# Main loop with eight batches to a body instead of two, and the end of the angle features at later steps

## The reference

```
def _chunk_attn(...):                       # layers L0, L1, L3; L0 and L1 are followed by add and norm
    scores = einsum('bnqhd,bnkhd->bnhqk', qh, kh) * scale + mask   # chunks of 64, 8 heads
    out = einsum('bnhqk,bnkhd->bnqhd', softmax(scores), vh)
    return (out @ W_out.T + b_out) * masks

idx = top_k(2 p.p - xx - xx^T, 30)          # p: the context's positions; 30 nearest of 1024
rel = pts[idx] - pts                        # three coordinates of each neighbour
r2, sxy2 = ...; rho = sqrt(r2); sxy = sqrt(sxy2)
theta = arctan2(zr, sxy); phi = arctan2(yr, xr)
feat = concat(sph, sph - mean(sph))         # sph = (rho, theta, phi)
h = lrelu(bn(lrelu(bn(lrelu(bn(feat @ W1.T)) @ W2.T)) @ W3.T))   # batch norms over all 32 batches
att = softmax(h over the 30 neighbours)
out = norm(x + layers + sum(att * xk))
```

## Time and profile before

| | us |
|---|---|
| median of 3 runs (lowest to highest) | 6258.06 (6256.48 to 6260.03) |
| the profiled execution | 6258.18 |
| its span in the trace | 6256.4 |
| DVE busy | 5585.7 (89%) |
| PE busy | 5448.7 (87%) |
| ACT busy | 4490.2 (72%) |
| POOL busy | 3506.1 (56%) |

### The profile page before, as it was taken

One profiled execution on the slowest core, in us unless ns is written; L12 is line 12 of the kernel. 1 busy time (PEld: TensorE's weight loads), 2 busy tenths in 40 slices (PEclk: granted clock), 3 DMA queues, 4 the chain that ended last, 5 costly groups with the idle time before them and its releaser, 6 DMA issues. The chain is left out here.

```text
span 6256.4 us, 228198 instructions
## 1 busy us (share of the span) xinstructions
PE 5448.7 (87%) x82804; PEld 3392.0 (54%) x82804; DVE 5585.7 (89%) x7936; ACT 4490.2 (72%) x17146; POOL 3506.1 (56%) x3600
## 2 busy tenths in 40 slices
PE   7888888888888888888888888888859769999999
PEld 3455555555555555555555555555533357777776
DVE  7999999999999999999999999999945787777776
ACT  7888888888888888888888888888845623333333
POOL 4466666666666666666666666666670033333332
PEclk9999999999999999999999999999969889999999
DMA  2333333333333333333333333333323023333332
GB/s 46 95 94 110 90 99 98 94 97 95 95 107 98 96 108 91 100 98 93 97 92 99 107 98 94 110 90 100 88 101 75 0 72 96 85 88 85 89 93 72
DMA packets 656108, 568.86 MB, mean 91 GB/s; under 512 B 557824, under 2 KB 579584, under 8 KB 620960
## 3 DMA queue, kind: packets, MB, share of 16 engines
q1 hardware_dynamic: 618016, 284.53, 19.4%
q10 hardware_dynamic: 36864, 268.45, 12.1%
HBM read 384.78 MB, written 67.24 MB: 72 GB/s over the span
## 5 line engine op out<-in xcount | busy, mean ns | idle before, releaser
L769 ACT ACTIVATE prob<-SC,row_max 128x64 f32<-128x64 f32 x6144 | 1836.1, 335 | 376.6 <-DVE row_max L1123 368.0
L886 POOL TENSOR_TENSOR prob<-prob,row_rec 128x512 f32<-128x512 f32 x768 | 800.6, 1042 | 1379.4 <-DVE row_rec L1131 1369.3
L769 ACT ACTIVATION_READ_ACCUMULATOR prob<-SC,row_max 128x1 f32 x6144 | 1387.0, 228 | 0.0
L1115 DVE FIND_INDEX8 nbr<-top,dist 128x8 uint16<-128x1024 f32 x1024 | 1234.5, 1217 | 0.0
L1108 DVE MAX8 top<-dist 128x8 f32<-128x1024 f32 x1024 | 1190.4, 1203 | 1.5
L1110 DVE MATCH_REPLACE8 dist<-top,dist 128x1024 f32<-128x1024 f32 x768 | 923.6, 1207 | 0.0
L627 PE MATMUL SC<-k_bd,q_t 128*64 128x256 f32 x6144 | 877.4, 409 | 0.0
L1801 ACT ACTIVATE dense<-DM 128x512 f32<-128x512 f32 x512 | 305.4, 596 | 750.1 <-PE DM L1760 750.0
L1909 DVE TENSOR_TENSOR d_oh_a<-lo,iota_a 128x4096 bf16<-128x4096 bf16 x256 | 583.8, 2290 | 241.2 <-PE DM L1760 240.3
L648 PEld LDWEIGHTS PT<-ident,prob 128*128 128x128 f32 x3072 | 358.0, 144 | 791.9 <-issue 770.4
L589 PEld LDWEIGHTS G<-table,low_all 128*128 128x128 bf16 x24576 | 664.8, 96 | 169.1 <-issue 92.5
(11 more groups left out here) (216 smaller groups left out, 9463.1 us busy)
## 6 DMA issues: line engine op xcount, KB each, us to landing
low_all<-low_scratch ACTq DMA_DIRECT2D x256, 1024.0 KB, 4.8
k_bd<-k_t SPq DMA_DIRECT2D x3072, 16.0 KB, 1.9
placed<-compact SPq DMA_DIRECT2D x256, 192.0 KB, 3.9
ctx<-in_ctx SPq DMA_DIRECT2D x32, 512.0 KB, 3.3
mask<-in_mask SPq DMA_DIRECT2D x32, 512.0 KB, 8.8
xb<-in_x SPq DMA_DIRECT2D x32, 512.0 KB, 3.4
x_scratch<-xb SPq DMA_DIRECT2D x32, 512.0 KB, 4.0
y_scratch<-y_b SPq DMA_DIRECT2D x32, 512.0 KB, 6.7
```

Of the source, the lines that this page charges most:

```text
L769: last = act.activation(prob[:, s % 4, g * CHUNK:(g + 1) * CHUNK], SC[:, s % 2, g * CHUNK:(g + 1) * CHUNK], ACT.Exp, bias=row_max[:, s % 2 ...
L886: pool.tensor_tensor(pr, pr, row_rec[:, r % 2, :].unsqueeze(2).to_broadcast([128, 8, CHUNK]), ALU.mult).then_inc(normed, 1)
L1115: last = dve.max_index(nbr[:, uu % BPB, t, k * 8:(k + 1) * 8], best, row)
```

## The change

`BPB` becomes 8, and `BUFS` = 2 takes its place wherever it meant the number of buffers; `TURNS` = 4 is how often a body goes round them. The written-out first and last bodies now have 8 batches each, and the loop has 2 bodies of 8: it jumps back once. No spurious batch -1 arises, so the waits on `gram_ready` lose their 1. The turn moves from step 44 to 45, the signed angle from 45 to 46 and its DMA from 46 to 47, the centring from 46 to 50.

```diff
 KEY_BUFS = 3
-BPB = 2
+BPB = 8
+BUFS = 2
+TURNS = BPB // BUFS
 BODY = N // BPB
...
-RATIO_AT, ANGLE_AT, TURN_AT, SPH_AT, SPH_OUT_AT = 44, 44, 44, 45, 46
-RHO_OUT_AT, TYPICAL_AT, CENTRE_AT, GRAM_AT = 39, 42, 46, 54
+RATIO_AT, ANGLE_AT, TURN_AT, SPH_AT, SPH_OUT_AT = 44, 44, 45, 46, 47
+RHO_OUT_AT, TYPICAL_AT, CENTRE_AT, GRAM_AT = 39, 42, 50, 54
...
-        ctx = sb("ctx", [128, BPB, T])
+        ctx = sb("ctx", [128, BUFS, T])
...
-            eng.wait_ge(arrivals[u % BPB], START + (i + u // BPB + 1) * 16)
+            eng.wait_ge(arrivals[u % BUFS], START + (i * TURNS + u // BUFS + 1) * 16)
...
-            act.wait_ge(gram_ready, START + N + 1)
+            act.wait_ge(gram_ready, START + N)
...
-                    pool.wait_ge(gram_ready, START + b + 1)
+                    pool.wait_ge(gram_ready, START + b)
```

More of the change, by code:

```diff
@@ L220, in attention_and_neighbours @@
         oh_b = sb("oh_b", [128, NF, 8], BF16)
-        pts = sb("pts", [128, BPB, 3 * NT])
-        table = sb("table", [128, BPB, 3, 24], BF16)
+        pts = sb("pts", [128, BUFS, 3 * NT])
+        table = sb("table", [128, BUFS, 3, 24], BF16)
         left = sb("left", [128, 2, 24])
@@ L252, in attention_and_neighbours @@
         zeroed = sem("zeroed")
[L253 to L256, removed]
+        ctx_in = [sem(f"ctx_in{u}") for u in range(BUFS)]
+        x_in = [sem(f"x_in{u}") for u in range(BUFS)]
+        mask_in = [sem(f"mask_in{u}") for u in range(BUFS)]
+        by_chunk_in = [sem(f"by_chunk_in{u}") for u in range(BUFS)]
         pj_ready = sem("pj_ready")
@@ L260, in attention_and_neighbours @@
         cols_out = sem("cols_out")
-        cols_in = [sem(f"cols_in{u}") for u in range(BPB)]
-        pts_in = [sem(f"pts_in{u}") for u in range(BPB)]
+        cols_in = [sem(f"cols_in{u}") for u in range(BUFS)]
+        pts_in = [sem(f"pts_in{u}") for u in range(BUFS)]
         pool_split = sem("pool_split")
@@ L283, in attention_and_neighbours @@
         applied = [sem(f"applied{j}") for j in range(2)]
-        x2_out = [sem(f"x2_out{u}") for u in range(BPB)]
+        x2_out = [sem(f"x2_out{u}") for u in range(BUFS)]
         y3_out = sem("y3_out")
@@ L396, in mask_by_chunk @@
                                  chunks[h].broadcast_to([32, PAIRS, CHUNK])).then_inc(by_chunk_in[u], 16)
-            for u in range(BPB):
+            for u in range(BUFS):
                 sp.wait_ge(zeroed, START)
@@ L540, in _ @@
             alone(sp)
-            for u in range(BPB):
-                sp.wait_ge(x2_out[u], START + BODY * 16)
+            for u in range(BUFS):
+                sp.wait_ge(x2_out[u], START + N // BUFS * 16)
             sp.wait_ge(y3_out, START + N * 16)
@@ L573, in projection @@
                     for e in range(2):
-                        last = pe.matmul(bank[64 * e:64 * e + 64, m * 64:(m + 1) * 64], ctx[:, pu % BPB, t0:t0 + CHUNK],
+                        last = pe.matmul(bank[64 * e:64 * e + 64, m * 64:(m + 1) * 64], ctx[:, pu % BUFS, t0:t0 + CHUNK],
                                          w_v[:, e, :, :], start=True, stop=True)
@@ L588, in fetch @@
                     for part in range(3):
-                        last = pe.matmul(G[:, g * 24:(g + 1) * 24], hot[:, t % 2, col:col + 128], table[:, v % BPB, part, :],
+                        last = pe.matmul(G[:, g * 24:(g + 1) * 24], hot[:, t % 2, col:col + 128], table[:, v % BUFS, part, :],
                                          start=(part == 0), stop=(part == 2))
@@ L697, in square @@
                     act.wait_ge(dist_row_ready, START + i * BPB + ub)
-                act.activation(sq[:, :], ctx[:, ub % BPB, :], ACT.Square).then_inc(squared, 1)
+                act.activation(sq[:, :], ctx[:, ub % BUFS, :], ACT.Square).then_inc(squared, 1)
             def squares(i, ub, h):
@@ L849, in split_row @@
             def split_row(i, ub, part, prior):
-                row = dist_row[:, ub % BPB, :]
+                row = dist_row[:, ub % BUFS, :]
                 if prior is None:
@@ L912, in step @@
                     landed(pool, mask_in, i, uu)
-                    pool.tensor_tensor(mine, mine, mask[:, uu % BPB, half], ALU.mult).then_inc(y_masked, 1)
+                    pool.tensor_tensor(mine, mine, mask[:, uu % BUFS, half], ALU.mult).then_inc(y_masked, 1)
                 if real(i, r, STEPS) and r % 4 == 3 and place(r)[0] < 2:
@@ L1114, in neighbours @@
                             alone(dve)
-                        last = dve.max_index(nbr[:, uu % BPB, t, k * 8:(k + 1) * 8], best, row)
+                        last = dve.max_index(nbr[:, uu % BUFS, t, k * 8:(k + 1) * 8], best, row)
                         if op == "i3":
@@ L1184, in indices @@
                 alone(dve)
-                here = nbr[:, v % BPB, :, :].rearrange("p t k -> p (t k)")
+                here = nbr[:, v % BUFS, :, :].rearrange("p t k -> p (t k)")
                 dve.tensor_scalar(low_u[:, :], here, 127, None, ALU.bitwise_and)
```

58 lines of the change are left out of this document (29 added, 29 removed).

## The result

| | median, us (lowest to highest) | profiled execution | its span |
|---|---|---|---|
| before | 6259.05 (6256.48 to 6262.41), 4 runs | 6258.18 | 6256.4 |
| after | 6201.8 (6193.92 to 6206.81), 4 runs | 6204.94 | 6203.1 |

The ratio is 0.9907, with a 95% interval of 0.989 to 0.9924: 57 us are gained. The forecast was 6153 us and its range ended at 6200, so the sign was right, the size was half, and the time lies 1.8 us outside the range.

The account below looks back on a forecast made before the run. DVE, 96% busy over batches 2 to 31 of the first part, was taken as the bound. Savings of 36 + 49 + 12 + 8 = 105 us from 6258.2 gave 6153 us, range 6124 to 6200.

Parts of the forecast that it names:

- The ratio: POOL, step 20: with the turn behind it, 1.27 us in all batches instead of 2.91 in even ones.
- The step-22 waits: First part, DVE waiting for ACT's exponentials and the gap behind: 49 us saved of 53.9, bounds 29 to 54.
- The jumps: First part's loop: 12 of 13 jumps back saved at 3.0 us each, 36 us, ends 17 and 45.
- straight code: First part: twelve more batches written out with constants in their waits, shortening step 22's wait; counted within that step's 49 us.
- Scores in step 23: First part, DVE's row_max waiting for PE's scores: 0.4 us less in 30 waits, 12 us, ends 0 and 24.
- L1162's extra: DVE's comparison in step 20 loses its extra 0.56 us in 14 odd batches: 8 us, ends 0 and 8.
- Centring collides: Rival: moved centring overlaps DVE's comparison in step 2 of a batch, costing 17 us: 6170 us, chance 0.05.
- The two other parts unchanged: Expected sign: the kernel's second and third parts stay as they were; no size given.
- The slower rival: First part: PE's instruction fetches miss once a batch in straight code, costing 138 us: 6291 us, chance 0.03.

Follow-up runs that it names:

- later steps only: Kernel before, still two batches to a body, with turn, angle and its DMA at steps 45, 46, 47 and centring at 47: 6231.11 us, ratio 0.9957.
- bodies of eight only: Kernel after with turn, angle and centring back at their old steps 44, 45, 46: 6271.14 us, ratio 1.0022 to before.
- run 9: Kernel after with the centring at step 47 instead of 50: 6200.8 us.
- Runs 1 and 2: Unused semaphore increments on PE ahead of the third part: 92 in the kernel after, 6158.12 us; 164 in the kernel before, 6301.72 us.

## Why the prediction was right, and where it failed

*The ratio.* Right. With the turn behind it it takes 1.27 us in all batches, and DVE's comparison, now L1164, 1.26; later steps only shows the same 1.27, bodies of eight only doesn't, so it is the later steps that do it, and of what they move only the turn stood ahead of the ratio. The step-22 waits gave 53.9 - 7.3 = 46.6 us, 49 were named; what is left is 16 waits of some 0.5 us, one in each batch of the loop, where I had the odd ones at 0. The mechanism holds for the remaining overlap, but why before was slow in even batches only is still not explained: with bodies of eight and the old steps it was slow in all.

*The jumps.* The 12 that went are worth about 34 us by DVE's waits, 36 were named: of 76.4 us for scores 42.5 are left, 33.9 less. Bodies of eight alone gave 39.6 us in the first part, with a little from straight code in it.

*Scores in step 23.* Wrong, 12 us were named. The one jump left takes 3.8 us of the 42.5, so step 23 has some 39 where before had 37: the whole drop is that of the jumps. What PE started sooner, DVE arrived sooner too, and the clock gave nothing: 0.96 instead of 0.95 over the stretch. It is the lower end of the term's bounds, 0.

*L1162's extra.* Right: over batches 2 to 31 its busy time fell from 347.7 to 339.0 us, 8.7, where 8 were named. But DVE's busy time as a whole fell by 20.5 us, from 4142.9 to 4122.4, where it was to stay otherwise the same. By lines, DVE's other instructions are together only some 2 us shorter, so where the last 10 went is open. The 12 us that nobody had named happen to make up for the 12 of step 23. So the sum for the first part, 105, met 100.6 in part by luck: 33.9 + 46.6 + 0 + 20.5 = 101.

*Centring collides.* No: run 9 moved it and nothing followed.

*The two other parts unchanged.* This is the step that failed, and it is a sentence in the list of signs, not a term of the sum: the third part had no term at all. Its 44.9 us separate forecast and result: 6153 + 44.9, with 4.4 for the first part and 2.5 for the second, is 6204.8, the time of the profiled execution (6204.94) within rounding. Runs 1 and 2 show their cause. I had treated code that isn't edited as code that doesn't change. But the change made PE's stream longer ahead of it, and its loop sits at a place in the instruction blocks that this sets.

*The slower rival,* that straight code starves PE, looked for the right resource in the wrong place. It asked whether the 24 written-out batches would be fetched in time. In the first part they were (3.7 us of stops in 5 places on PE; 14 more gaps without a releaser, of 2.1 us each, stand where the loop's batches wait 2.1 us for ACT's `v_b`), and the price fell due behind the 13 jumps of a loop that no line of the change touches. The earlier trace rows already had the price of a fetch that isn't ahead; I didn't ask which other loops pay it. Had I looked at that one, the row of its branch, 3.9 us, and the 2.8 us of stops beside the 4.6 us of the first loop's would have hinted that before was near its best case, with something to lose and little to win; how much, 44.9 / 13 = 3.5 us a jump, only the runs show.

The range ended at 6200 because it held only doubts about the first part. A term of 13 jumps by 0 to 3.5 us for the place of the third loop, unknown without a count of PE's instructions, would have put it at 6153 to 6198 from that alone.

## What to carry to other kernels

A change that adds or removes instructions moves every loop behind it on that engine: count from a loop's target to the end of its block of 256, and price each jump back by it, here up to 3.5 us. Before such a change is judged, try its loops moved by padding (92 increments gave 44 us here) or written out (115 us for both loops). And where two waits follow one another on the busiest engine, curing one alone moves part of it to the next: here the halves gave 67 us and the whole 101.

## What the runs showed of the hardware

- A jump back on PE costs by where its target lies: 3.9 to 4.7 us for the branch at the median, and another 0.4 to 2.5 us of stop at the next block end, if this is 20 to 131 instructions away. At 251 there is none. Where PE has to wait for the next block, it goes on 3.9 to 4.7 us after the branch's end, of which some 0.9 us is the block's packet. Together with the lower clock after it this is 45 us in 13 jumps: PE's granted clock is 0.50 in the first 4.4 us after a jump in both kernels (0.61 behind the first of before); in the next 7 us it is 0.90 to 1.00 in before, and 0.67 to 0.81 in after, where PE has stopped once more in between. Over the third part it is 0.94 instead of 0.96, with 12.5 us more of PE busy.
- At a jump DMA is busy as well: in the 4.4 us behind the one shown above the data queues move 251 GB/s at a share of 0.95. But this isn't what makes the stop. Before has 246 GB/s at a share of 0.94 in the 4.4 us behind its own jump and no stop, and the packet of the next block takes 0.88 to 0.96 us there in both kernels, where the shortest of the whole queue takes 0.88.

```profile
5570.60:5575.00 4.40, 2.85 (x42) 2.70 (x42) 0.00 (x0) 1.02 (x1) 0.00 (x0) 0.50 0.95 251
```

- In a loop ACT's table load stands behind the wait for POOL; in straight code, where the wait is on a constant, it runs ahead of it, and 1.3 us of it is hidden. Of bodies of eight only, in the loop and behind it:

```profile
1540.94 1.28 ACT L829 ACT_TABLE_LOAD   x1 [4.26 <-POOL apart L1034]
```
```profile
4100.03 1.28 ACT L829 ACT_TABLE_LOAD   x1
...
4104.11 0.63 ACT L829 ACTIVATE angle<-apart 128x512 f32<-128x512 f32 x1 [2.79 <-POOL apart L1034]
```

DVE's wait in step 22 is 2.82 us in the first and 1.46 in the second. This is what batch 30 showed in the earlier trace rows, which the prediction put down to straight code without saying how.
- Open: the alternation of the slow ratio before, whether the place of the loop's end sets the branch's own time, where some 10 us of DVE's busy time in the first part went, and why the first part of the same code ends anywhere within 13 us.
